# Three long softmax attentions on one core: V made inside the attention, the first key load in two parts, row maxima spread over seven banks and over slots

## What is computed

```python
q, k, v = h @ Wq, h @ Wk, h @ Wv             # (2048, 128); 16 heads of 8 features
s = scale * einsum('qd,kd->qk', q[h], k[h])  # per head, 2048 x 2048
p = softmax(s, axis=-1)                      # att1, att2: causal; att0: over all keys,
z = p @ v                                    # and p is masked to k >= q only after the softmax
```

## Time and profile before

| | us |
|---|---|
| median of 3 runs (2616.67 to 2623.15) | 2621.33 |
| profiled execution, whole | 2619.61 |
| its span (first to last instruction) | 2617.6 |
| att0: first tile, first exponential, last exponential's start | 96.4, 146.8, 788.7 |
| att1: first tile, first exponential, last exponential's start | 919.8, 968.1, 1356.2 |
| att2: first tile, first exponential, last exponential's start | 1652.3, 1700.6, 2088.6 |

### The profile page before, as it was taken

One profiled execution on the slowest core, in us unless ns is written; L12 is line 12 of the kernel. 1 busy time (PEld: TensorE's weight loads), 2 busy tenths in 40 slices (PEclk: granted clock), 3 DMA queues, 4 the chain that ended last, 5 costly groups with the idle time before them and its releaser, 6 DMA issues. The chain is left out here.

```text
span 2617.6 us, 40655 instructions
## 1 busy us (share of the span) xinstructions
PE 2235.2 (85%) x14536; PEld 1008.3 (39%) x14544; DVE 1773.8 (68%) x3947; ACT 1517.4 (58%) x2345; POOL 361.0 (14%) x562
## 2 busy tenths in 40 slices
PE   4599999999994499999976996799999768979797
PEld 2344433444332143333333442333333334734473
DVE  5688888888834578787744555787778368437643
ACT  1068888888882028887742221188876533943592
POOL 3100000000000200011120002000011224303330
PEclk8589999999997659999987997599999888989897
DMA  4510200000000531010100003420101024613560
GB/s 155 100 30 7 33 8 11 13 7 13 4 4 2 133 49 27 11 29 15 29 17 1 0 0 109 62 36 12 28 12 27 21 80 155 216 35 129 169 186 17
DMA packets 78881, 130.26 MB, mean 50 GB/s; under 512 B 16496, under 2 KB 38768, under 8 KB 77168
## 3 DMA queue, kind: packets, MB, share of 16 engines
q1 hardware_dynamic: 75392, 117.62, 17.4%
q10 hardware_dynamic: 3312, 10.33, 1.4%
HBM read 53.13 MB, written 15.20 MB: 26 GB/s over the span
## 5 line engine op out<-in xcount | busy, mean ns | idle before, releaser
L794 ACT ACTIVATE att_probs<-psum 128x1024 f32<-128x1024 f32 (+3 forms) x1152 | 1035.1, 959 | 244.7 <-PE psum L846 242.8
L736 DVE TENSOR_REDUCE att_part_max<-psum 128x1 f32<-128x512 f32 x1312 | 840.8, 685 | 167.5 <-PE psum L828 165.4
L828 PE MATMUL psum<-k_rows,att_q_rows 64*128 64x512 f32 (+3 forms) x2304 | 739.5, 489 | 100.8 <-DMA att_q_rows<-q_pieces 60.5
L828 PEld LDWEIGHTS psum<-k_rows,att_q_rows 64*128 64x128 f32 x2304 | 350.9, 197 | 653.4 <-DVE att_part_max L736 279.3
L846 PE MATMUL psum<-att_q_rows,k_rows 64*128 64x512 f32 (+3 forms) x2304 | 453.0, 416 | 27.9 <-ACT att_probs L794 18.0
L871 PE MATMUL psum<-att_probs,v_aug 128*9 128x512 f32 (+3 forms) x3712 | 432.2, 539 | 0.5 <-POOL att_probs L674 0.3
L780 ACT ACTIVATE att_rise<-psum 128x512 f32<-128x512 f32 x240 | 144.4, 602 | 309.0 <-PE psum L828 275.4
L846 PEld LDWEIGHTS psum<-att_q_rows,k_rows 64*128 64x128 f32 x2304 | 237.2, 190 | 177.7 <-ACT att_probs L794 160.7
L733 DVE CUSTOM_DVE_ANT_0 att_masked<-psum,mask_max_sb 128x128 bf16<-128x128 f32 (+3 forms) x512 | 232.8, 485 | 54.7 <-PE psum L828 52.8
L725 DVE CUSTOM_DVE_ANT_0 att_rise<-psum,att_rise 128x512 f32<-128x512 f32 x240 | 166.1, 692 | 78.1 <-PE psum L828 49.1
L674 POOL TENSOR_SCALAR_AFFINE_SELECT att_probs<-att_probs 128x256 f32<-128x256 f32 x256 | 102.5, 406 | 800.3 <-ACT att_probs L794 797.7
(11 more groups left out here) (256 smaller groups left out, 2138.4 us busy)
## 6 DMA issues: line engine op xcount, KB each, us to landing
lproj_swapped<-lproj_other SPq DMA_DIRECT2D x128, 128.0 KB, 2.1
k_rows<-k_pieces SPq DMA_DIRECT2D x48, 320.0 KB, 10.9
latt_k<-local_k_T SPq DMA_DIRECT2D x32, 384.0 KB, 3.0
att_q_rows<-q_pieces SPq DMA_DIRECT2D x168, 64.0 KB
lproj_table<-in_tables SPq DMA_DIRECT2D x16, 512.0 KB, 4.2
latt_q<-local_q_T SPq DMA_DIRECT2D x32, 256.0 KB, 2.4
latt_v_seen<-local_v_tok SPq DMA_DIRECT2D x64, 128.0 KB, 2.4
latt_v_seen<-local_v_tok SPq DMA_DIRECT2D x32, 256.0 KB, 2.4
```

Of the source, the lines that this page charges most:

```text
L736: nc.vector.tensor_reduce(column, ring[e % NRING][:, 0:w], AX.X, ALU.max).then_inc(ring_free, 1)
L794: nc.scalar.activation(probs[s % NPROBS][:, pr, :, at:BANK], st[pr][:, :, at:BANK], ACT.Exp, scale=scale).then_inc(st_free, 1)
L828: nc.tensor.matmul(ring[e % NRING][:, 0:w], q_rows[u % NQ][rows, pr, qt * P:(qt + 1) * P].bitcast(F32R), k_rows[b][rows, pr, (kc + 1) * BA ...
```

## The change

1. **V moves.** `project` makes no V. At the start of `attention` PE makes all of V (16 matmuls into banks 0 to 3), and DVE copies it into `v_aug` behind its memsets, while the q and k loads run.
2. **First k load in two parts.** Of unit 0's keys the first 1024 columns (k1 - k0 and k0; 4 DMAs of 128 KB) are issued first under a semaphore of their own, `k_begun`; the other 1536 columns (4 DMAs) follow and are waited for at the first tile that needs them (`plan.beyond`, entry 32). The next group's k now goes ahead of unit 2's queries.
3. **Seven banks in the opening.** Entries of the opening use banks 4, 5, 6, 0, 1, 2, 3 in turn. Before the first scores PE waits until the last tiles in banks 0 to 3 are taken (`last_in`).
4. **Unit 0's tiles** stand in a new order: two rises, then the two k0 tiles, for all 16 rows, and then the rest. The opening has 19 rises where it had 11.
5. **Slots.** Tiles are put into one slot per step (`slots_of`, `cut`). Where a unit would leave steps empty, tiles are cut evenly over them (units 3, 7 and 11 of att1 and att2 have 2 to 4 tiles in nearly every step). The stream of units 1 to 14 of att0 is as it was. Rises in att1 and att2: 60 for 56 each, in att0 136 for 128, by the 8 more of unit 0.
6. **The last turn** is raised into the list one place earlier, ahead of the products of the first step of unit 14.
7. **The last unit's keys** (att1, att2) go to columns 0 to 511 of `k_rows1`, loaded when unit 5 is done.
8. **Two `probs` buffers** in place of three, and products of step s-1 in place of s-2; the copy of z (L770) one step earlier accordingly.
9. `part_max` is set to -1e30 again for each unit (14 more memsets an attention); `masked` buffers are counted by masked tiles; one more `clear_semaphores` after att0.

```diff
-AHEAD = 4
+HEAD = 16
 NRISE = 2
 RISE = -1
-NPROBS = 3
+NPROBS = 2
...
-            for t in range(NT):
-                if t % 4 == 0 and t >= 8:
-                    pe.wait_ge(v_free, t // 4 - 1)
-                m = nc.tensor.matmul(v_ps[t // 4 % 2][:, t % 4 * P:(t % 4 + 1) * P], h_T[:, t * P:(t + 1) * P], wv, start=True, stop=True)
-                if t % 4 == 3:
-                    m.then_inc(v_full, 1)
...
+            if self.causal and u == len(self.units) - 1:
+                b = 1
+                free = max(v for v in range(u) if self.units[v][1] > 1 and self.k_of[v][0] == b)
+                self.k_loads.append((g, b, 0, BANK, BANK, free))
+                self.k_of.append((b, sum(load[1] == b for load in self.k_loads), 0))
...
+                first = 0 if chunks > 2 else BANK
+                if u == 0:
+                    first = 2 * BANK
+                self.k_loads.append((g, b, first, first, (chunks + 1) * BANK - first, last_use))
...
+        for u in range(1, NU):
+            more = HEAD if u + 1 < NU else 0
+            total = tiles_of(u) - HEAD + more
+            if total < 4 * self.blocks[u - 1] - HEAD or (total < 4 * self.blocks[u - 1] and more):
+                bodies[u] = round(self.blocks[u - 1] * (tiles_of(u) - HEAD) / total)
+                heads[u + 1] = self.blocks[u - 1] - bodies[u]
...
+        raised = lambda counts: [n + (n == last and (m == 0 or counts[m - 1] == last)) for m, n in enumerate(counts)]
+        after, before = raised(after), raised(before)
...
+        self.bank = [(4, 5, 6, 0, 1, 2, 3)[e % 7] if e < self.opening else 4 + (e - self.opening) % NRING for e in range(len(self.stream))]
+        self.earlier = [max((x for x in range(e) if self.bank[x] == self.bank[e]), default=None) for e in range(len(self.stream))]
...
+        if u == 0:
+            tiles = [(*r, kc, i) for r in rows for kc in (RISE, 0) for i in range(2)]
+            tiles += [(*r, kc, i) for kc in range(2, chunks) for r in rows for i in range(2)]
+            tiles = [tiles[n:n + 4] for n in range(0, len(tiles), 4)]
+            return [(four[0:2], four[2:4]) for four in tiles[:heads]], [(four[0:2], four[2:4]) for four in tiles[heads:]]
...
+            eights = 2 * chunks if bodies is None else HEAD // 8
+            upper, lower = ([(*r, kc, i) for r in rows for kc in range(chunks)] for i in range(2))
+            lower = [tile for tile in lower if tile[:2] not in rows[:eights] or tile[2] > 1]
+            slots = []
+            for n, r in enumerate(rows[:eights]):
+                a, d, f, h = upper[4 * n:4 * n + 4]
+                e, g = lower[2 * n:2 * n + 2]
+                slots += [([a, (*r, RISE, 1)], [(*r, 0, 1), d, e]), ([f, g], [h])]
+            rest = [tile for pair in zip(upper[4 * eights:], lower[2 * eights:]) for tile in pair]
+            return self.cut_ahead(slots, heads), slots[4:] + self.cut(rest, bodies or 0)
...
+    def cut(self, tiles, count):
+        slots = []
+        for n in range(count):
+            mine = tiles[len(tiles) * n // count:len(tiles) * (n + 1) // count]
+            slots.append((mine[:2], mine[2:]))
+        return slots
...
+            load_k_part(plan.units[0][0], 0, 0, 0, 2 * BANK, k_begun)
             load_k(0)
+            load_k(1)
             load_q(2)
-            load_k(1)
...
+            for c in range(NC):
+                dve.wait_ge(v_full, c + 1)
+                to = v_aug[:, 4 * c:4 * c + 4, :, 0:HD]
+                ps = v_ps[c][:, :].rearrange("p (t h d) -> p t h d", t=4, d=HD)
+                if bv is not None:
+                    by_head = bv[:, :].rearrange("p (h d) -> p h d", d=HD)
+                    nc.vector.tensor_tensor(to, ps, by_head.unsqueeze(1).to_broadcast([P, 4, NH, HD]), ALU.add).then_inc(v_done, 1)
+                else:
+                    nc.vector.tensor_copy(to, ps).then_inc(v_done, 1)
...
+                if u + 2 < NU:
+                    nc.vector.memset(part_max[u % 2][:, :, :], NEG).then_inc(parts_set, 1)
...
-                if u > 0 and kb == 2:
+                if u > 0 and kb == 1:
...
+                            if u == 0:
+                                pe.wait_ge(k_begun, KIN)
+                            else:
+                                pe.wait_ge(k_in[b], KIN * nth)
+                        if e == plan.beyond:
                             pe.wait_ge(k_in[b], KIN * nth)
-                        if e >= NRING:
-                            bank_free(e - NRING)
+                        if plan.earlier[e] is not None:
+                            bank_free(plan.earlier[e])
...
+            for t in range(NT):
+                m = nc.tensor.matmul(v_ps[t // 4][:, t % 4 * P:(t % 4 + 1) * P], h_T[:, t * P:(t + 1) * P], wv, start=True, stop=True,
+                                     skip_group_check=True)
+                if t % 4 == 3:
+                    m.then_inc(v_full, 1)
             maxima(plan.opening)
+            for e in plan.last_in:
+                bank_free(e)
             for s, (u, kb) in enumerate(steps):
                 if kb == 0:
                     pe.wait_ge(m_in[u % NQ], MIN_ * (u // NQ + 1))
                 scores(s, 0)
                 scores(s, 1)
                 maxima(plan.before[s])
-                if s >= 2:
-                    products(s - 2)
+                if s >= 1:
+                    products(s - 1)
                 maxima(plan.after[s])
-            products(NS - 2)
             products(NS - 1)
...
+        clear_semaphores(nc, first_sem)
```

More of the change, by code:

```diff
@@ L491, in __init__ @@
+        for u, (first, second), turn in slots:
+            for tiles in (first, second):
+                if tiles is second and turn:
                     self.turn_at.append(len(self.stream))
                     self.stream.append((u - 1,))
-                for tile in second:
-                    self.stream.append((u, *tile))
-                before.append(len(self.stream))
-            self.done_at.append(len(self.stream))
-        self.turn_at.append(len(self.stream))
-        self.stream.append((len(self.units) - 1,))
```

187 lines of the change are left out of this document (105 added, 82 removed).

## The result

The changed kernel takes 2534.79 us, median of 4 runs (2533.88 to 2539.44), the kernel before beside it 2620.66 (2616.67 to 2623.15): ratio 0.968, 95% interval 0.966 to 0.969. That is 86 us less, where 56 were forecast and 75 was the far end of the range. The sign was right, the size was not, and of the mechanisms some were right and some were missing.

What follows compares the result with a forecast made beforehand. PE bounds att0's steady part, DVE and ACT close behind, so gains lie elsewhere: att0 10.6, att1 21.5, att2 24.8, less 1 for semaphores, together 55.9 off 2619.6, so 2563.7; as median 2565 us, range 2546 to 2598.

Steps and rivals of the forecast that it cites:

- the opening: From first tile to first scores: seven banks let PE run ahead, summing to 44.7 us, 3 us less per attention.
- the first scores: From first scores to first exponential in each attention: the prediction had no term here, forecast 0.
- the lag: Products of step s-1 in place of s-2, with two probs buffers, in the steady steps: taken as 0.
- the even slots: Tiles moved from full to empty steps in att1 and att2: net 2.7 us less each, bounds 0 and 6.
- V and the first load: Start of each attention: moving V saves 0.3 us in att0, the first tile comes 8 us sooner in each.
- The estimate of 11 us: Wait for the first load: 1.2 MB at 125 GB/s plus 1.6 us, in place of 19.4 us.
- The first rival: The first load comes no sooner, taking back 24 us: 2589 us, chance 0.12.
- Steady steps: Regular steps: memsets clearing maxima cost 0.7 us in att0, 1 us each in att1 and att2; changed product order 0.
- The ends: Units 12 to 14 of att1 and att2: earlier last keys and raised turn save 8.8 and 12.1 us.
- The second rival: Ends keep half their loss, waiting for the last unit's maxima instead of keys: 12 less gained, 2577 us, chance 0.15.
- Clearing semaphores: The added clearing of semaphores after att0: costs 1 us.
- The rivals: Products wait for POOL, slower, 2661 us, chance 0.05; more in flight wakes PE's clock in the opening, 2559, chance 0.10.

## Why the prediction was wrong

Step by step, as the prediction put them. The terms that failed are the opening, the first scores, the lag and the even slots.

- **V and the first load.** The number was right, 24 us forecast and 23.5 measured, the mechanism only in part, and that they agree so well is luck: the split is worth 27.9, and 4.4 of it went elsewhere. The prediction had the queries wait for their turns beside SP's long pieces. One run that takes the split away (+27.9 in the waits) and one that goes further (-4.7) show that what SP has in flight makes the first tile late. But the keys were nearly as late as the queries before, and in att1 and att2 the first tile now waits for keys; whether shorter pieces or fewer bytes did it stays open. The estimate of 11 us also counts the start twice, since its rate of 125 GB/s already spans the whole wait. The first rival is excluded. The rule beside it, a fixed cost of about 2 us for a DMA, stands in the Trainium skill ("DMA: Bandwidth & Descriptors", Anatomy of one DMA) for DMAs that GpSimd issues; here SP and ACT issue them. The runs show only that the split pays for its four more DMAs, not what these cost. V's part was taken at 0.3 us; the first issue came between 75.9 and 77.4 us in the kernels measured, 76.93 before, so nothing can be said of 0.3.
- **The opening.** The mechanism was right, the term was mis-sized: 3 us each, measured 4.8, 7.6 and 7.6. In att0 the sum of 44.7 us was 1.8 too long: 0.4 in the 16 reductions of two tiles (12.3 for 12.7; each takes DVE 0.61 us, and every second one waits some 0.2 to 0.3 for ACT's relu), 0.5 in the 32 single ones and the rest in unit 1's tiles. The larger error was to use att0's sum for all three. In att1 and att2 masked tiles are narrower and DVE has 35.0 us of work, not 39.3. Before, that brought little, for the opening was bound by the round through three banks as much as by DVE; the sentence that DVE sets the pace was only half true. With seven banks it counts in full.
- **First scores.** Left out altogether: 1.28 us of table load and a relu left the path in each attention, 5.2 us in all. It was to be seen in the trace of before, between the first scores and the first exponential.
- **Steady steps.** The clears were taken at 2.7 us in all and cost nothing that shows. The lag was counted 0, from the path of the products alone. I looked at who waits for POOL and PE, and not at what else the change of lag moves on ACT: the copy of z. Lag, buffers and copy together are worth 4.5 us in att0 and some 2 in att1, with nothing to show in att2. That the steps of att0 gained only 2.2 is mostly because its first unit takes 1.5 longer; why it does stays open.
- **The ends.** The number was right, its split was not: units 12 to 14 gained 8.2 and 11.6 us, forecast 8.8 and 12.1. The keys account for about 7, and for unit 13 too, of which the prediction gave the last gap to the turn. Putting the turn back costs 4 more, but in units 14 and 15. The second rival is out; its price of 12 us is also more than half of the forecast gain of 20.9 at the ends, which is 10.5.
- **Even slots.** The size was wrong and so was the view. Units 3, 7 and 11 gained 7.1 and 4.8 us, where 3.2 was forecast for them; evenness is worth 1.2 of it. In att1 2.4 of the 7.1 come with the lower clock that the kernel before had there, and no term of the prediction had it. I had divided whole halves of unit 7 by their steps and so averaged away that tiles on narrow steps cost more than tiles on wide ones. The new order of tiles in c = 1 units, 2 to 3 us, was in the diff and got no term.
- **Clearing semaphores** was put at 1 us; everything outside the three attentions took 3.3 more, nearly all of it (3.9) between att0 and att1. In the two traces 1.7 of it is there by the first matmul of the next norm, which comes 24.4 us behind att0's last exponential where it came after 22.7, and 1.7 more comes within that norm. No run took it apart.
- **The rivals** on POOL and on the clock: products waited 3.2 us in all; the clock stayed at 0.50 through all three openings, although the tiles now go back to back. By the rule of the Trainium skill ("TensorE: Matmul & The Clock Gate", What's actually happening), activity releases the throttle. The trace doesn't bear it out in the openings, with PE shown busy 38.8 of 42.9 us at 0.50; it agrees in the first steps, where the clock rises to 1.00 after 7.8 busy of 8.1 us.

## What to carry to other kernels

When two queues share the DMA engines, look at what stands in the other queue before you touch the one that is late, and at how much has to land before the first work can start: splitting the first load on SP's side halved the wait of the first tile, though that wait ended on ACT's queue. When a lag or a position in a list changes, list everything that moves with it on every engine, the small copies too, and give each slot the price of that slot (narrow or wide, with a relu or without) and not of an average over its unit. And where three like stages differ in their tiles, work the sum out for each.

## What the runs showed of the hardware

- ACT loads its function table where its next exponential stands in the program, not when the scores come: 1.28 us, over 1.7 us ahead of att0's first exponential in the changed kernel and on the path before the change and with three banks.
- TensorE's clock stayed at 1.2 GHz for 38 to 43 us in which PE is shown busy 34.4 of 38.2 and 38.8 of 42.9 us, and after a stall of 4.9 us it was 0.64 of full speed on the mean of the next unit. It rose to 2.4 GHz 8.1 us after att0's first scores.
- A part of the program that no edit touches took 537.5 us in one execution, with a lower granted clock, and 526.8 to 530.2 in all the others.
